# Four-layer graph kernel on one Trainium2 core: the layers' VectorE programs without loops, some masks moved to VectorE, unread TensorE products, another tail of the neighbour maximum

## The chip, the cores and the metric

The kernel runs on one core of a Trainium2 chip. Its time is the device time of one execution in microseconds (us); lower is better. Three runs of the kernel before gave 5988.77 us in the median, 5978.95 and 5993.84 at the ends. The profile is one further execution, traced by the hardware profiler. Engines: PE is TensorE (matrix products, with PEld its weight loads), DVE is VectorE, ACT is ScalarE, POOL is GpSimd, SP is SyncE, which here only issues DMAs.

## The reference

There are N = 8192 nodes with 128 features and a symmetric 0/1 adjacency `adj` of 8192 x 8192 int32 with about 0.4% of ones. Four layers follow one another, each as `x = layernorm(x + layer(x))`:

```
L0: out[i] = max over neighbours j of x[j]        (0 where a row has no neighbour)
L1: h = x @ W;  e = leaky_relu(h@a_src [:,None] + h@a_dst [None,:], 0.2)
    att = softmax(where(adj > 0 and sum(h) != 0, e, -1e9))
    att kept only where att >= 1e-4, times the number of valid neighbours
    out = elu(h + att @ h)
L2, L3: h = x @ W;  the same e;  att = softmax(where(adj > 0, e, -big));  out = elu(att @ h)
```

## The kernel before, in words

**Neighbour maximum** (`neighbour_max`). Rows of `adj` come in 64 tiles of 128 rows, four pieces of 1 MB each (`adjb`, SP's queue). PE transposes a tile in 64 blocks, ACT turns them into 0/1 bytes (`stage`) and stores them as the mask `mask_t` that the later layers read. DVE works out for every row which neighbours are to be gathered one by one, POOL gathers them from a copy of x (`x_ext`) into `ring`, DVE reduces them into `nm` (which is `X`). For the others, PE multiplies "lone" masks with x split in three bf16 parts (`xs`); each product of two blocks is a *pair* (L548): DVE keeps the running maximum `top`. Tiles go in *quads* of four: 16 quads (NC) of 32 pairs; pairs of quad q run beside the tiles of quad q+1, and those of the last quad alone, in a last stretch without new tiles. x itself is loaded in four quarters at the start, by SP, ahead of the second tile's rows; DVE splits them (`SPLIT_BEHIND`: quarter 0 behind tile 1, quarters 1 and 2 behind tile 2, quarter 3 behind tile 3). After the last pair DVE finds each row's lowest value over all 64 tiles (L706), does a few small steps on [128, 64], POOL reduces one flag over the partitions (L352), and DVE and SP read it and branch: if it is set, a slow exact loop runs (it is not set for these inputs). Then `first_norm`, a block of its own, loads x again (SP), multiplies nm by "has neighbours", adds x (L767) and takes the rows' statistics (L769, L772).

**A layer** (`attention_layer`) has a preparation and a main block. In the *preparation* PE transposes X in 16 groups g of four blocks (L886), ACT copies them to `XT` (L909), and PE multiplies them with three columns (L877, four groups behind). In layers 1 and 2 DVE normalises X first (L924, from stats that ACT turned into rstd). In layers 2 and 3 DVE sums all of XT (`zc`, L951) once the last group is copied, and then the preparation ends with a few small steps.

The *main block* goes over 16 chunks c of 512 columns, and in each over 64 tiles j. For each j DVE makes a weight tile `w` = max(q, E[j]) * mask (L1503 in layers 2 and 3; in layer 1 `u` from the threshold theta, L1478, and then w, L1489), in a ring of 8 tiles, and PE multiplies it with GX (L1258). At fixed j (36 and 48 in layer 1, 24, 28 and 38 in layers 2 and 3) DVE handles the results of the chunk before (`post`, `post_rest`, `standardise`).

Layer 1 also needs theta of chunk c+1 while chunk c is multiplied. For each of its 64 tiles PE *lifts* scores (two products of 512 columns, L1186 and L1187, into one of two banks), ACT makes a 0/1 mask of them (`above`, a ring of ten slots, L1322), and PE multiplies masks in batches of eight with `kg` and `km` (L1194, L1196). After the 64th ACT and PE work out theta (L1344 is its last step). For chunk 0 this happens alone, ahead of everything (PE `ahead_of(0, 0, [0, 0], T)`), while DVE has only GX to weigh (L1462); for the others PE mixes it between the products of chunk c.

**What sets the order.** Every engine's program is in order; semaphores link them. In the layers' main blocks the chunks 1 to 14 are a hardware loop of two chunks each on every engine (`chunks`), with chunk 0 and chunk 15 outside. In such a loop a wait's value stands in a register: `Tally` adds to it (L134) and `hold` waits on it (L78) and bumps a spare semaphore. `Steps` waits on constants. The neighbour maximum is written out without loops on PE, ACT and DVE.

## Time and profile before

| | |
|---|---|
| median of three runs | 5988.77 us (5978.95 to 5993.84) |
| profiled execution | 6010.32 us; its trace spans 6008.3 us |
| busy: PE, DVE, ACT, POOL | 5075.2 (84%), 4748.3 (79%), 2028.6 (34%), 1186.8 us (20%) |
| PE's granted clock, mean | 0.922 of 2.4 GHz |
| neighbour maximum with its tail and the first norm | 0 to 2316.7 us |
| layer 1: preparation, theta of chunk 0, the chunks | 2316.7, 2380, 2445 to 4037 us |
| layer 2: preparation, the chunks | 4037, 4091 to 5026 us |
| layer 3: preparation, the chunks | 5026, 5071 to 6008 us |

The stages can be told apart by lines: a stage is between the first and last instruction of its lines. The clock has two levels, 1.2 and 2.4 GHz, and is given as a share of 2.4 GHz: 0.50 is the lower level all the time.

### The profile page before, as it was taken

Reading aid. Unit: us, or ns where it says so; the run is one execution under the profiler, and the core shown is the slowest. Engines: PE = TensorE matmul, PEld = TensorE weight load, DVE = VectorE, ACT = ScalarE, POOL = GpSimd, SP = SyncE. Lnnn points to the kernel's source line nnn. Section 1 sums busy time; section 2 is a strip of 40 time slices with the busy share of each in tenths; the row PEclk is TensorE's granted clock in tenths of the full one; section 3 lists DMA queues with packets and bytes.
Section 4 is the critical chain, followed back from the end, with each engine's and each line's share of the span. In section 5 each row is a group of like instructions: output and inputs, shape, how many; then the busy total and the mean of one; then the engine's idle time right before and its main releaser. Section 6 shows DMA issues by size and latency. Waiting matters only on the chain. (4 is left out here: it accounts for less than half of the span.)

```text
span 6008.3 us, 91716 instructions
## 1 busy us (share of the span) xinstructions
PE 5075.2 (84%) x24003; PEld 2392.2 (40%) x24113; DVE 4748.3 (79%) x8829; ACT 2028.6 (34%) x2862; POOL 1186.8 (20%) x1368
## 2 busy tenths in 40 slices
PE   4777767667677674899999999979999998999999
PEld 3333333333333332344444444435444445444444
DVE  6676766667666665699989998988888886888888
ACT  3444444444444441555555555510000001000000
POOL 5555454454444540000000000000000000000000
PEclk6888888888888885999999999998999998999999
DMA  7555555555555522011111111011222211221211
GB/s 256 191 189 190 188 187 180 178 189 187 184 185 181 184 94 85 29 43 44 44 43 43 44 44 44 29 44 63 72 76 74 73 49 71 74 82 67 89 60 35
DMA packets 149498, 628.30 MB, mean 105 GB/s; under 512 B 29360, under 2 KB 37936, under 8 KB 91632
## 3 DMA queue, kind: packets, MB, share of 16 engines
q1 hardware_dynamic: 78432, 482.58, 23.0%
q0 software_dynamic: 33744, 73.21, 4.1%
q10 hardware_dynamic: 36864, 67.13, 3.2%
q8 instruction: 200, 3.28, 0.2%
q14 instruction: 258, 2.11, 0.1%
HBM read 551.42 MB, written 75.56 MB: 104 GB/s over the span
## 5 line engine op out<-in xcount | busy, mean ns | idle before, releaser
L1258 PE MATMUL bank<-w,GX 128*128 128x512 f32 x6144 | 2777.6, 597 | 41.9 <-DVE w L1489 22.3
L1258 PEld LDWEIGHTS bank<-w,GX 128*128 128x128 f32 x6144 | 1145.6, 190 | 1398.2 <-issue 1340.4
L1503 DVE SCALAR_TENSOR_TENSOR w<-q,E,m 128x512 f32<-128x512 f32 x2048 | 1455.0, 758 | 170.0 <-PE bank L1258 92.0
L306 POOL DMA_INDIRECT ring<-x_ext,idx x1051 | 1030.4, 980 | 1098.1 <-DVE X L560 338.4
L450 PE MATMUL sums<-lone,xs 128*128 128x512 fp8e4 x3000 | 852.3, 427 | 300.9 <-DVE top L548 204.3
L548 DVE TENSOR_TENSOR top<-top,sums 128x1024 f32<-128x1024 f32 x484 | 589.8, 1219 | 645.2 <-remote 378.2
L375 ACT ACTIVATE stage<-tp 128x1024 fp8e4<-128x1024 uint16 x512 | 523.9, 1025 | 1089.9 <-remote 634.7
L1478 DVE SCALAR_TENSOR_TENSOR u<-theta,E,m 128x512 fp8e4<-128x512 f32 x1024 | 765.9, 749 | 98.3 <-issue 84.9
L1322 ACT ACTIVATE above<-bank,offset 128x512 fp8e4<-128x512 f32 x1024 | 649.0, 684 | 529.3 <-PE bank L1187 527.0
L1489 DVE SCALAR_TENSOR_TENSOR w<-q,E,u 128x512 f32<-128x512 f32 x1024 | 760.6, 744 | 74.9 <-PE bank L1258 74.8
L450 PEld LDWEIGHTS sums<-lone,xs 128*128 128x128 bf16 x3000 | 295.2, 106 | 827.4 <-issue 619.0
L362 ACT ACTIVATE lone<-first_ps 128x1024 fp8e4<-128x1024 f32 x512 | 522.1, 1020 | 91.4 <-remote 41.8
L436 PE MATMUL first_ps<-stage,firsts 128*128 128x512 fp8e4 x1022 | 343.2, 421 | 126.3 <-ACT lone L362 99.0
L417 PE MATMUL tp<-ident_b,adjb 128*128 128x128 bf16 x4096 | 361.4, 237 | 76.7 <-issue 40.5
L1187 PE MATMUL bank<-m,lift 128*128 128x512 fp8e4 x1024 | 390.1, 381 | 7.3 <-ACT parts L1300 1.1
L1186 PE MATMUL bank<-parts,three 128*128 128x512 bf16 x914 | 348.5, 381 | 13.0 <-ACT above L1322 12.9
L1134 POOL TENSOR_TENSOR lone_part<-mean_w,nohas 128x512 f32<-128x512 f32 x32 | 37.8, 1185 | 1626.6 <-DVEq L1429 1608.7
L1273 ACT ACTIVATE num<-bank 128x512 f32<-128x512 f32 x48 | 28.4, 592 | 890.9 <-PE bank L1258 890.9
L417 PEld LDWEIGHTS tp<-ident_b,adjb 128*128 128x128 bf16 x4096 | 278.1, 107 | 111.0 <-issue 54.3
L429 PE MATMUL tally<-powers,stage 128*128 128x16 bf16 x4096 | 171.4, 171 | 157.9 <-ACT stage L375 112.6
L429 PEld LDWEIGHTS tally<-powers,stage 128*128 128x128 fp8e4 x4096 | 164.5, 99 | 286.0 <-ACT stage L375 143.5
L553 DVE TENSOR_TENSOR ring<-ring 128x128 f32<-128x128 f32 (+2 forms) x448 | 248.2, 554 | 2.6 <-issue 0.2
(231 smaller groups left out, 3018.2 us busy)
## 6 DMA issues: line engine op xcount, KB each, us to landing
adjb<-in_adj SPq DMA_DIRECT2D x256, 1024.0 KB
m<-mask_t SPq DMA_DIRECT2D x192, 1024.0 KB, 4.9
mask_t<-stage ACTq DMA_DIRECT2D x256, 256.0 KB
ring<-x_ext,idx POOLq DMA_INDIRECT x1051
out<-X SPq DMA_DIRECT2D x16, 256.0 KB, 2.4
Wn<-in_L_gnn_W SPq DMA_DIRECT2D x3, 64.0 KB, 1.9
A<-in_L_gnn_a SPq DMA_DIRECT2D x6, 0.5 KB, 2.1
X<-in_x SPq DMA_DIRECT2D x4, 0.5 KB, 22.3
```

The source lines that it names most:

```text
L306: pool.indirect_dma_start(ring[:, s, :], None, x_ext, bass.IndirectOffsetOnAxis(ap=idx[:, k, s:s + 1], axis=0)).then_inc(done, 16)
L362: nc.scalar.activation(lone[:, b, :, :], first_ps[:, :, :], ACT.Relu, saturate=False).then_inc(lone_made, 1)
L375: nc.scalar.activation(stage[:, q, e * TRB:(e + 1) * TRB, k * P:(k + 1) * P], tp[e % 2][:, :, :].bitcast(U16), ACT.Sign, saturate=False).t ...
L417: last = nc.tensor.transpose(tp[e % 2][:, i, :], low_half[:, j // PW, j % PW:j % PW + P], ident_b[:, :])
L450: last = nc.tensor.matmul(out[:, a, :], xs[:, part_, 2 * n + a, :], lone[:, b, a, :], start=(part_ == 0), stop=(part_ == 2))
L548: nc.vector.tensor_tensor(out=top[:, :, :], in0=top[:, :, :], in1=sums, op=ALU.max).then_inc(sums_used, 1)
L1187: nc.tensor.matmul(out[:, :], lift[:, :], m[:, b, j, :], start=False, stop=True).then_inc(lifted, 1)
L1258: last = nc.tensor.matmul(acc[b][:, :], GX[:, j, :], w[:, j % WR, :], start=(j == 0), stop=(j == T - 1))
L1322: nc.scalar.activation(above[:, j % AR, :], lift_ps[j % 2][:, :], ACT.Sigmoid, bias=offset[:, j:j + 1], saturate=False).then_inc(g_made, 1)
L1478: nc.vector.scalar_tensor_tensor(out=u[:, j % 4, :], in0=theta[:, b, :], scalar=E[:, j:j + 1], in1=m[:, b, j, :], op0=ALU.is_le, op1=ALU.m ...
L1489: nc.vector.scalar_tensor_tensor(out=w[:, j % WR, :], in0=q, scalar=E[:, j:j + 1], in1=u[:, j % 4, :], op0=ALU.max, op1=ALU.mult).then_inc ...
L1503: nc.vector.scalar_tensor_tensor(out=w[:, j % WR, :], in0=q, scalar=E[:, j:j + 1], in1=m[:, b, j, :], op0=ALU.max, op1=ALU.mult).then_inc( ...
```

## The change

- The chunks of DVE's main programs in all three layers are written out as Python loops (`written_out`), and so are ACT's; their registers become constants (`Count` for `Tally`). PE, POOL and SP keep their loops.
- In layer 1 some of the `above` masks are made by DVE (`own_mask`), straight from q, E and the mask, with no lifted scores on PE and nothing on ACT: 32 of 64 (the odd ones) for chunk 0, and tiles 8, 24, 40 and 56 for each later chunk, made behind w tiles 12, 24, 34 and 46 of the chunk before. For chunk 0 DVE weighs three eighths of GX ahead of its masks and the rest behind them.
- In each preparation PE gets products that nobody reads (`keep_warm`, 256 bf16 columns each): 20 at the start, 8 behind group 1, 4 behind each of the groups 2 to 15, and 4 behind each of the next three groups' score products; 96 in all.
- At the start, quarters of x are loaded ahead of the rows of the tile behind which DVE splits them, not all ahead of tile 1.
- At the tail of the neighbour maximum, `first_norm` is gone. SP loads x again (into `adjb`) once the last tile is transposed; DVE takes the lowest value quad by quad behind pairs 8 to 22 of the last quad; POOL adds x to each of those 15 quads as it is released; DVE does the last quad itself; ACT writes the flag. DVE takes the statistics before it reads the flag. The multiplication by "has neighbours" moves into the branch.

```diff
+LOWEST_AT = 8
+WARM = 4
+WARM_UP = 20
+WEIGHED_FIRST = 3
+OWN_FIRST = tuple(range(1, T, 2))
+OWN_AT = {12: 8, 24: 24, 34: 40, 46: 56}
+OWN = tuple(OWN_AT.values())
...
+def own_tiles(c):
+
+    return OWN_FIRST if isinstance(c, int) and c == 0 else OWN
...
+class Count:
+
+    def __init__(self, eng, sem, start=0):
+        self.eng, self.sem, self.at, self.n = eng, sem, start, 0
+
+    def wait(self, n=1):
+
+        self.at += n
+        if self.at > 0:
+            self.eng.wait_ge(self.sem, self.at)
...
-            for k in range(XQ):
-                quarter = slice(k * T // XQ, (k + 1) * T // XQ)
-                sp.dma_start(nm[:, quarter, :], x.rearrange("(t p) f -> p t f", p=P)[:, quarter, :]).then_inc(x_in[k], 16)
-            with sp.Fori(1, T) as t:
+
+            def rows(t):
+
                 for h in range(PIECES):
 
                     hold(sp, transposed, (t - 1) * 8 + (h + 1) * HT)
                     sp.dma_start(adjb[:, h, :], adj[bass.ds(t * P, P), h * PW:(h + 1) * PW]).then_inc(adj_in[h], 16)
 
+            for t in range(1, TC):
+                for k in SPLIT_BEHIND[t]:
+                    quarter = slice(k * T // XQ, (k + 1) * T // XQ)
+                    sp.dma_start(nm[:, quarter, :], x.rearrange("(t p) f -> p t f", p=P)[:, quarter, :]).then_inc(x_in[k], 16)
+                rows(t)
+            with sp.Fori(TC, T) as t:
+                rows(t)
+
+            sp.wait_ge(transposed, T * 8)
+            sp.dma_start(x_again, x.rearrange("(t p) f -> p t f", p=P)).then_inc(x_back, 16)
...
+            pool.wait_ge(x_back, 16)
+            for quad in range(NC - 1):
+                at = slice(quad * TC, (quad + 1) * TC)
+                pool.wait_ge(rows_step, quad + 1)
+                nc.gpsimd.tensor_tensor(out=nm[:, at, :], in0=nm[:, at, :], in1=x_again[:, at, :], op=ALU.add).then_inc(x_added, 1)
...
+            act.wait_ge(missed_shared, 1)
+            nc.scalar.activation(flag[:, :], missed_all[:, :], ACT.Copy).then_inc(flag_ready, 1)
...
+            def lowest_of(quad):
+
+                at = slice(quad * TC, (quad + 1) * TC)
+                rows_done.did(nc.vector.tensor_reduce(lowest[:, at], nm[:, at, :], axis=AXX, op=ALU.min))
+
+            def between(n):
+
+                if n == LOWEST_AT:
+                    dve.wait_ge(top_used, NC - 1)
+                    dve.wait_ge(lower_free, T - TC + 1)
+                    dve.wait_ge(rest_free, T - TC + 1)
+                if LOWEST_AT <= n < LOWEST_AT + NC - 1:
+                    lowest_of(n - LOWEST_AT)
+
+            def row_statistics():
+
+                rows_done.settle()
+                dve.wait_ge(x_added, NC - 1)
+                for t in range(T):
+                    rows_done.did(nc.vector.bn_stats(bn[:, t, :], nm[:, t, :]))
+                rows_done.settle()
+                for t in range(T):
+                    rows_done.did(nc.vector.bn_aggr(stats[:, t, :], bn[:, t, :]))
+                rows_done.settle()
...
                     if quad is not None:
                         pair(quad * 32 + 8 * k + e, 8 * k + e, quad == NC - 1)
+                    if quad == NC - 1:
+                        between(8 * k + e)
...
-            dve.wait_ge(lower_free, T + 1)
-            dve.wait_ge(rest_free, T + 1)
             merge(NC - 1)
             take_top(NC - 1)
             dve.wait_ge(top_used, NC)
-            lowest = junk
-            steps.do(nc.vector.tensor_reduce(lowest, nm[:, :, :], axis=AXX, op=ALU.min))
+            steps.settle()
+            side.settle()
             steps.did(nc.vector.scalar_tensor_tensor(out=due[:, :], in0=due[:, :], scalar=TOP_BIT, in1=found[:, :], op0=ALU.mult, op1=ALU.not_equal))
+            lowest_of(NC - 1)
+            rows_done.settle()
+            dve.wait_ge(x_back, 16)
+            last = slice(T - TC, T)
+            rows_done.did(nc.vector.tensor_tensor(out=nm[:, last, :], in0=nm[:, last, :], in1=x_again[:, last, :], op=ALU.add))
...
-            dve.wait_ge(missed_shared, 1)
-            nc.vector.tensor_copy(flag[:, :], missed_all[:, :]).then_inc(flag_ready, 1)
+            steps.do(nc.vector.tensor_scalar(nohas[:, :], deg[:, :], 0.0, None, ALU.is_equal))
+            row_statistics()
...
-def first_norm(nc, x, X, deg, nohas, stats):
...
+                def keep_warm(number):
+
+                    halves = ident[:, :].bitcast(BF16)
+                    for _ in range(number):
+                        nc.tensor.matmul(banks[5][:, 0:2 * P], halves[:, 0:P], halves, start=True, stop=True)
+
+                keep_warm(WARM_UP)
                 for g in range(NG):
...
                     if g >= BEHIND:
                         scores(g - BEHIND)
+                    if g >= 1:
+                        keep_warm(2 * WARM if g == 1 else WARM)
                 for g in range(NG - BEHIND, NG):
                     last = scores(g)
+                    if g < NG - 1:
+                        keep_warm(WARM)
...
+        def written_out(chunk, end, say_last=False):
+
+            for c in range(NC):
+                if say_last and c == NC - 1:
+                    chunk(c, c % 2, False, True)
+                else:
+                    chunk(c, c % 2, c == 0)
+            end(NC - 1, 1)
...
                 while state[0] < scores or (scores == T and state[1] < T):
                     if state[0] < T:
-                        lifted_scores(c, b, state[0])
+                        if state[0] not in own_tiles(c):
+                            lifted_scores(c, b, state[0])
                         state[0] += 1
...
                 for j in range(T):
...
-                    above_free.wait()
-                    hold(act, lifted, c * T + j + 1)
-                    nc.scalar.activation(above[:, j % AR, :], lift_ps[j % 2][:, :], ACT.Sigmoid, bias=offset[:, j:j + 1], saturate=False).then_inc(g_made, 1)
+                    slots += 1
+                    if j in own_tiles(c):
+                        continue
+                    above_free.wait(slots)
+                    slots = 0
+                    hold(act, lifted, act_tiles_before(c, j) + 1)
+                    nc.scalar.activation(above[:, j % AR, :], lift_ps[lift_bank(c, j)][:, :], ACT.Sigmoid, bias=offset[:, j:j + 1], saturate=False).then_inc(g_made, 1)
...
-            w_free = Tally(dve, w_used)
-            post_steps = Tally(dve, post_step)
+            w_free = Count(dve, w_used)
+            post_steps = Count(dve, post_step)
...
+            def own_mask(c, b, j):
+
+                hold(dve, q_ready, c + 1)
+                hold(dve, mask_in[b][j // QJ], wait_of(c, b))
+                hold(dve, g_used, c * T + j + 1)
+                nc.vector.scalar_tensor_tensor(out=above[:, j % AR, :], in0=qb[:, b, :], scalar=E[:, j:j + 1], in1=m[:, b, j, :],
+                                               op0=ALU.is_le, op1=ALU.mult, saturate=False).then_inc(own_made, 1)
...
                 if first:
-                    for i in range(T // GXP if cut else 1):
+                    for i in range(WEIGHED_FIRST if cut else 1):
                         weigh(i)
                 hold(dve, q_ready, c + 1)
                 if cut:
+                    if first:
+                        for j in OWN_FIRST:
+                            own_mask(0, 0, j)
+                        for i in range(WEIGHED_FIRST, T // GXP):
+                            weigh(i)
...
+                        if j in OWN_AT and not last_chunk:
+                            own_mask(c + 1, 1 - b, OWN_AT[j])
...
-            chunks(dve, chunk, end, True)
+            written_out(chunk, end, True)
```

## Rows read from the trace of the kernel before

**Rows 1.** Stretches (stretch, length, then busy us and count of each engine, clock, DMA):

```profile
2317.00:2380.00 63.00, 41.14 (x195) 40.20 (x196) 27.91 (x118) 12.13 (x23) 0.53 (x3) 0.50 0.34 135
...
2445.00:4037.00 1592.00, 1526.93 (x6309) 646.87 (x6414) 1449.14 (x2352) 806.13 (x1366) 42.33 (x80) 0.99 0.11 38
```

**Rows 2.** Timeline, start of the program (start, length, engine, line, count, idle before and releaser):

```profile
3.01 29.09 SPq L262 DMA_DIRECT2D X<-in_x  x4
...
41.74 1.89 PE L417 MATMUL tp<-ident_b,adjb 128*128 128x128 bf16 x16 [22.49 <-DMA adjb<-in_adj]
...
53.48 0.69 DVE L598 TENSOR_TENSOR keys<-tally,opens 128x512 int32<-128x512 int32 x1 [13.65 <-ACT opens L368]
```

**Rows 3.** Timeline, last pairs of the neighbour maximum to the preparation:

```profile
2238.25 1.22 DVE L548 TENSOR_TENSOR top<-top,sums 128x1024 f32<-128x1024 f32 x1 [0.51 <-PE sums L450]
...
2253.58 8.69 DVE L706 TENSOR_REDUCE stats<-X 128x64 f32<-128x8192 f32 x1
...
2263.54 0.38 POOL L352 PARTITION_ALL_REDUCE missed_all<-missed  x1 [46.98 <-DVE missed L711]
...
2272.15 0.20 DVE L763 TENSOR_SCALAR nohas<-deg 128x64 f32<-128x64 f32 x1 [8.04 <-PEq L164]
...
2298.20 11.89 DVE L769 BATCH_NORM_STATS2 bn<-X 128x6 f32<-128x128 f32 x61
...
2316.70 0.06 DVE L930 MEMSET epsc<- 128x1 f32 x1 [1.68 <-PEq L102]
```

**Rows 4.** POOL's line 1134, all of it (duration min/median/max ns, first and last start):

```profile
L1134 POOL TENSOR_TENSOR lone_part<-mean_w,nohas x32: 1147/1155/1478, 4098.4 to 5899.9; 128x512 f32<-128x512 f32 x32
```

**Rows 5.** Timeline, preparations of layers 1 and 3:

```profile
2320.79 1.97 PE L886 MATMUL bank<-ident,X 128*128 128x128 f32 x8 [67.97 <-DVE X L924]
...
5036.70 0.60 ACT L909 ACTIVATE XT<-bank 128x512 f32<-128x512 f32 x1 [0.69 <-PE bank L886]
...
5057.78 0.60 ACT L909 ACTIVATE XT<-bank 128x512 f32<-128x512 f32 x1 [1.86 <-PE bank L886]
5058.48 8.69 DVE L951 TENSOR_REDUCE zc<-XT 128x1 f32<-128x8192 f32 x1 [26.81 <-ACT XT L909]
```

**Rows 6.** Timeline of ACT, layer 1, masks of chunk 0:

```profile
2426.22 5.43 ACT L1322 ACTIVATE above<-bank,offset 128x512 fp8e4<-128x512 f32 x8 [0.74 <-PE bank L1187]
2432.46 4.04 ACT L1322 ACTIVATE above<-bank,offset 128x512 fp8e4<-128x512 f32 x6 [0.82 <-PE bank L1187]
```

**Rows 7.** ACT's line 1344, theta, all of it:

```profile
L1344 ACT ACTIVATE theta<-bank x16: 597/597/598, 2444.4 to 3931.9; 128x512 f32<-128x512 f32 x16
```

**Rows 8.** Timeline, three thetas of layer 1 and DVE between the second and third:

```profile
2639.56 0.60 ACT L1344 ACTIVATE theta<-bank 128x512 f32<-128x512 f32 x1 [1.07 <-PE bank L1224]
...
2738.28 0.60 ACT L1344 ACTIVATE theta<-bank 128x512 f32<-128x512 f32 x1 [1.04 <-PE bank L1224]
...
2744.60 1.41 DVE L1478 SCALAR_TENSOR_TENSOR u<-theta,E,m 128x512 fp8e4<-128x512 f32 x2 [4.97 <-issue]
...
2838.42 0.60 ACT L1344 ACTIVATE theta<-bank 128x512 f32<-128x512 f32 x1 [1.04 <-PE bank L1224]
```

**Rows 9.** The page's costliest groups: line 1187 (busy us, mean ns, idle before):

```profile
L1187 PE MATMUL bank<-m,lift 128*128 128x512 fp8e4 x1024 | 390.1, 381 | 7.3 <-ACT parts L1300 1.1
```

**Rows 10.** Timeline, layer 2, DVE after the results of a chunk, PE behind it:

```profile
4234.50 0.69 DVE L1439 SCALAR_TENSOR_TENSOR X<-hp,X 128x512 f32 x1 [0.25 <-DVE hp L1437]
...
4236.67 6.71 DVE L1503 SCALAR_TENSOR_TENSOR w<-q,E,m 128x512 f32<-128x512 f32 x10
...
4237.57 2.81 PE L1258 MATMUL bank<-w,GX 128*128 128x512 f32 x6 [0.46 <-DVE w L1503]
```

**Rows 11.** The chain that ended last, layer 3 (start, length, what):

```profile
5162.49 0.86 PE bank L1151 x2
...
5219.88 0.86 PE bank L1151 x2
...
5277.91 0.86 PE bank L1151 x2
```

82 lines of the change are left out of this document (46 added, 36 removed).

## The prediction

> **What bounds the kernel now.** I read the stretches first [rows 1]: they say which engine is full in which stage and at which clock. In layer 1's chunks PE is busy 1526.93 of 1592 us and DVE 1449.14 of 1592, so PE is the bound there with DVE close behind. In its preparation PE is busy 41.14 of 63 us at a clock of 0.50. Then I read the timeline where one stage meets the next, since there engines take turns and every step is on the path: the tail of the neighbour maximum is DVE alone [rows 3], the masks of chunk 0 are an exchange between ACT and PE [rows 6]. Last, the chain that ended last, for the length of a chunk and what interrupts it [rows 11]. The change touches each of these places, so I price seven parts, in time saved on the path, against the profiled execution's 6010.32 us. It lies 21.6 us above the median of the runs, 5988.77 us; I take the saving off that median.
>
> **A. The start: 10 us.** SP is busy for 29.09 us with issuing four quarters of x, 7.3 us each, and only then issues tile 1's rows, for which PE sits idle 22.49 us [rows 2]. With one quarter ahead, they are issued 21.8 us earlier. What follows is DVE, which waits 13.65 us for tile 1's counts and has, from there, 29 us of work in one piece (two extractions and two splits). So at most 13.65 us go; nothing if the DMA engines are simply full (the copy of x into x_ext runs then). I take 10. The moved quarters stand ahead of rows of tiles 2 and 3, whose pieces wait for PE's transposes anyway.
>
> **B. The neighbour maximum's tail: 30 us.** From the lowest value's start to the preparation's first instruction is 2316.70 - 2253.58 = 63.1 us [rows 3]. What remains of it: the lowest value of one quad, 8.69 / 16 = 0.54, with its start 0.6; the last quad's addition, 0.7; six small steps, 1.5; from the statistics' start to the preparation 2316.70 - 2298.20 = 18.5; and the 8.04 us in which DVE reads the flag, branches and leaves the block, which now stand behind the statistics. Together 29.3, so 33.8 go (two passes of 8.69 over all rows and the wait for x, among others). Against it: 15 minima of 0.6 us, 9.0 us of DVE, now stand between pairs. There DVE idles 0.51 us a pair at the end [rows 3], and more before; but it also has the last reductions to do, and PE can run only two sums ahead. I take 3.5 us of delay (0 to 9). POOL's 15 additions cost some 1.16 us each by its nearest row [rows 4], 17 us, and lie in the 46.98 us in which POOL waits for nothing but DVE [rows 3]. If that cover were gone, the statistics would wait up to 17 us. The new load of x takes the place of adjacency rows that have run out. Net 30 (22 to 34).
>
> **C. Preparations: 17.5 us.** At the lower clock a group of four blocks takes 1.86 + 0.60 = 2.46 us; at full clock, which layer 3's preparation had for a short while behind unbroken transposes, 0.69 + 0.60 = 1.29 us [rows 5]. The unread products have no row. The nearest is the f32 transpose of 128 columns, 1.97 / 8 = 0.25 us at half clock [rows 5]; from the product of 512 columns, 0.38 us at full clock and overlapping its neighbours [rows 9], a 256-column one is at most 0.19. I take 0.22 at half and 0.11 at full clock (0 to 0.25: 0 where it hides behind weight loads). A group then takes 1.29 + 4 x 0.11 = 1.73 us, 0.73 less than now. The question is whether the clock rises. In this trace it stood at full where PE ran dense products, and at half in the preparations, where most products are the three-column ones. The twenty products at the start, and the four behind each group, are dense. I expect it to rise within the first groups and to stay. Twelve groups: 8.8 us. Layer 1: 8, with a little for the rise; the first 20 (4.4 us) hide while DVE normalises (4.1 us from 2316.70 to 2320.79). Layers 2 and 3 end by the sum over XT, 8.69 us, which starts with the last copied group [rows 5], so only what comes before that counts: 6.5 for layer 2, and 3 for layer 3, where X is ready at once, the 20 products stand ahead of everything, and three groups already ran at full clock.
>
> The Trainium skill ("TensorE: Matmul & The Clock Gate", section "What's actually happening") says that the gate opens by how busy the engine has been. Here the profile shows PE busy nearly without a break through the second half of that preparation at 0.50, so by the profile's busy time there would be nothing left for unread products to raise. By that rule they only add their own time; this is rival 1.
>
> **D. Theta of chunk 0: 21 us.** ACT makes eight masks in 2432.46 - 2426.22 = 6.24 us [rows 6]: 5.43 of work and a wait for a batch to free slots. With half of them on DVE, ACT has 2.7 us of work in a batch; DVE has 4 x 0.67 (the price of such an operation: 6.71 / 10 [rows 10]) = 2.7 beside it. The exchange remains: slots come free only with PE's batch. I put a batch at 3.6 us. Six batches at full clock save 15.8; the first two, at half clock and with PE's products the bound, some 2.6 each. Bounds: 8 x (6.24 - 3.1) = 25, and 12 if DVE, which starts behind three weighings (3.5 us), sets the pace. The five weighings behind the masks (6 us) lie beside the 7 us of small steps that lead to theta.
>
> **E. Layer 1's chunks: 32 us.** Fifteen thetas apart are 3931.9 - 2444.4 = 1487.5 us [rows 7], 99.17 each. Inside a loop round a chunk takes 2738.28 - 2639.56 = 98.72, with the jump back 2838.42 - 2738.28 = 100.14 [rows 8]: DVE stands for 4.97 us without a cause in the profile, and its ring of eight w tiles covers all but 1.4. Seven jumps on DVE: 10. Four tiles fewer to lift are 8 products of 512 columns; at 0.215 us (at most 0.38 [rows 9]) 1.72 us a chunk, 26 in all. DVE gets 4 x 0.67 = 2.7 us a chunk [rows 10]. In work per chunk, by the shares of [rows 1], DVE goes from 0.910 x 99.2 = 90.3 to 93.0 us and PE from 0.959 x 99.2 = 95.1 to 93.4. The two then sit side by side, so I take 4 off the 36: 32 (10 to 38). An own mask waits for its slot of `above`; behind it on DVE are w tiles, of which PE has up to eight in hand.
>
> **F. Layers 2 and 3: 17 us.** In every chunk PE runs dry once, 0.46 us, behind DVE's handling of the last chunk's results [rows 10]. In that stretch each dependent step of DVE starts 0.25 us after its predecessor, because its wait goes through a register; with constants I expect about 0.1, and with six such steps that is 0.9 us, enough to close the gap. 30 gaps of 0.46: 13.8. The jump back: 5277.91 - 5219.88 = 58.03 against 57.39 [rows 11], so 0 to 0.64 for each of fourteen; I take 3.5 in all. Then PE is full, and nothing is left.
>
> **G. Layer ends: 2 us**, for some five dependent steps of DVE at each of three ends, 0.15 each.
>
> Sum: 10 + 30 + 17.5 + 21 + 32 + 17 + 2 = 129.5 us; 5988.77 - 129.5 = 5859, which I give as 5860.
>
> **Rivals.**
> 1. The clock stays at half in the preparations. For it: PE's busy share there is already near full. Against: what fills it are weight loads. The products then cost 0.22 each: 76 in layer 1, 64 in layer 2 (up to the last copied group), 84 in layer 3, 49 us instead of a gain of 17.5. Time: 5860 + 66 = 5926.
> 2. DVE becomes layer 1's bound: its own masks and the waits for their slots eat what PE saves. For it: 93.0 and 93.4 us of work side by side. Against: DVE's steps get cheaper by constants. Then E is only the jumps, 10: 5882.
> 3. The two ends of the neighbour maximum absorb the edits: the start is bound by the DMA engines (A = 0), and the minima between pairs all count (9, not 3.5): 5860 + 10 + 5.5 = 5876.
> 4. Slower: the written-out programs of DVE stall where the loops did not. The stall of 4.97 us at a jump costs 1.4 us. Were there three such stalls in each of the 48 chunks, that is 144 x 1.4 = 202 us: 5860 + 202 = 6062. It decides from two in each chunk on (134 us). Against it: the chunks outside the loops already are straight code, on the same engines, and so is the neighbour maximum.
>
> **How the numbers follow.** Chances: my forecast 0.66, rival 1 0.12, rival 2 0.10, rival 3 0.09, rival 4 0.03. The parts' own bounds, taken together, give 5838 to 5890 around the forecast; rivals 2 and 3 lie within, and rival 1, with other parts at their better ends, reaches down to 5912. Range 5838 to 5912. 0.3% (18 us) is what a measurement of this kernel can tell from no change: faster 0.95, same 0.02, slower 0.03.
>
> **What would show it.** A: tile 1's first transposes near 20 to 32, not 41.74. B: a preparation that starts some 30 us sooner than by A alone, with POOL's additions done before the last pair. C: clock near 1 and copies of XT 1.7 us apart; 3.3 or so means rival 1. D: about 3.6 us a batch, theta 0 some 44 us into its stage, not 65. E: thetas 97 us apart without a long step every second chunk; 98.7 means rival 2. F: posts 56.9 us apart and no idle of PE ahead of L1258. The prediction is wrong if idle "issue" time shows up inside DVE's written-out chunks, or if the last pairs come over 9 us later.

## The result and the profile after

The changed kernel takes 5835.4 us (median of four runs, 5833.0 to 5839.7), the kernel before beside it 5987.3 us (5979.0 to 5993.8): ratio 0.9748, 95% interval 0.9736 to 0.9761. I had said 5860 with a range of 5838 to 5912. The direction was right, and so was the sign of every part that could be measured; the saving was 152 us instead of 129, and the time lies 2.6 us below the range. Run beside the kernel before on two chips once more, it had the ratio 0.9748 again (e5, e17 below).

The stages, from the start times of their first and last instructions in the two traces (epsilon's memset, the copy of sdh, the thetas). The profiled execution of before stood 23 us above the median of before, that of after at its own median. The stages from the preparations on agree to about 1 us from one execution to the next, apart from layer 1's preparation (up to 3 us, see e1 below); the neighbour maximum doesn't, so I put most of this excess there. Row A is therefore not read from the two traces but is the rest of the 151.9 us.

| stage | before | after | saved | forecast |
|---|---|---|---|---|
| A, neighbour maximum up to the last tile's counts | | | 8.7, as the rest | 10 |
| B, last counts to last pair | 87.5 | 89.5 | -2.0 | -3.5 |
| B, lowest value to preparation 1 | 63.1 | 22.3 | 40.8 | 33.8 |
| C, preparations 1, 2, 3 up to sdh | 48.3, 50.1, 41.0 | 38.6, 39.7, 37.1 | 9.8, 10.4, 3.8 | 8, 6.5, 3 |
| D, sdh to first theta | 79.4 | 59.5 | 19.9 | 21 |
| E, fifteen thetas | 1487.5 | 1452.3 | 35.1 | 32 |
| F and G, sdh to the stage's end, layers 2 and 3 | 938.5, 940.8 | 926.2, 928.9 | 12.3, 11.9 | 19 with the next |
| G, last theta to preparation 2 | 106.1 | 104.9 | 1.2 | |

Stretches of after, in order: the steady part of layer 1's preparation, layer 1's chunks, one chunk of layer 2 (stretch, length, busy us and count of PE, PEld, DVE, ACT, POOL, then PE's granted clock, DMA share, GB/s).

```profile
2262.00:2280.00 18.00, 18.00 (x173) 17.58 (x173) 6.78 (x27) 6.57 (x11) 0.00 (x0) 1.00 0.53 219
2345.00:3798.00 1453.00, 1420.90 (x6121) 613.03 (x6121) 1392.00 (x2248) 767.32 (x1301) 51.60 (x79) 1.00 0.12 42
4040.00:4097.00 57.00, 57.00 (x141) 25.67 (x140) 52.04 (x87) 3.04 (x6) 1.15 (x1) 1.00 0.21 74
```

Against [rows 1], the preparation is at clock 1.00 and no longer at 0.50, and PE has no idle time in this stretch of layer 2. (The same holds from 4000 to 4850 us in layer 2 and from 4960 to 5800 us in layer 3, where it is shown busy all the time.) Layer 1's chunks are 97.8% PE and 95.8% DVE.

The start, which answers to [rows 2]: SyncE, PE, DVE.

```profile
18.16 21.25 SPq L332 DMA_DIRECT2D X<-in_x  x2
39.46 5.50 SPq L327 DMA_DIRECT2D adjb<-in_adj  x4
...
26.26 1.89 PE L494 MATMUL tp<-ident_b,adjb 128*128 128x128 bf16 x16 [7.00 <-DMA adjb<-in_adj]
34.46 1.03 PE L494 MATMUL tp<-ident_b,adjb 128*128 128x128 bf16 x8 [6.31 <-DMA adjb<-in_adj]
...
44.04 0.69 DVE L704 TENSOR_TENSOR keys<-tally,opens 128x512 int32<-128x512 int32 x1 [4.18 <-ACT opens L443]
```

Tile 1's first piece comes at 26.26 instead of 41.74, DVE's wait is 4.18 instead of 13.65.

The tail, which answers to [rows 3]:

```profile
2224.91 0.68 DVE L655 TENSOR_REDUCE codes<-X 128x4 f32<-128x512 f32 x1
2225.62 0.69 DVE L816 TENSOR_TENSOR X<-X,adjb 128x512 f32<-128x512 f32 x1
...
2227.32 0.38 POOL L427 PARTITION_ALL_REDUCE missed_all<-missed  x1 [19.10 <-DVE missed L820]
2227.82 0.20 ACT L481 ACTIVATE flag<-missed_all 128x1 int32<-128x1 f32 x1 [8.11 <-POOL missed_all L427]
...
2242.88 1.26 DVE L674 BATCH_NORM_AGGREGATE stats<-keys 128x2 f32<-128x6 f32 x18
...
2247.16 0.06 DVE L1026 MEMSET epsc<- 128x1 f32 x1 [3.01 <-PEq L131]
```

From the last aggregate to the preparation 3.01 us pass, in which DVE reads the flag, branches and leaves the block. I had set down 8.04 us for these three, and 1.68 for leaving the block that is gone. The sequencers' own records, which the views above leave out, show why. Among them each engine has a DRAIN at the end of a block, ahead of the barrier at which the engines meet. Before:

```
2263.45  8.412 POOL DRAIN L164
2263.54  0.380 POOL PARTITION_ALL_REDUCE L352 missed_all<-missed
```

After:

```
2227.23  8.409 POOL DRAIN L219
2244.18  0.541 DVE TENSOR_LOAD L827 <-flag
2244.76  0.217 DVE FUSED_REGOPS L827
2245.08  0.072 DVE COMPARE_BRANCH L828
2245.68  0.063 DVE DRAIN L219
```

DVE has its flag in 1 us. GpSimd's drain at the block's end takes 8.4 us, and the block's barrier waits for it. Before, everyone waited: DVE had its flag at 2265.13 us and its own drain at 2265.29, GpSimd's drain ended at 2271.86, and DVE went on at 2272.15. Now the drain lies beside 16.8 us of statistics.

The preparation's groups, which answer to [rows 5]:

```profile
2262.63 0.42 PEld L969 LDWEIGHTS bank<-ident 128*128 128x128 bf16 x4
2262.74 0.60 PE L969 MATMUL bank<-ident 128*128 128x256 bf16 x4
2263.07 0.47 PEld L978 LDWEIGHTS bank<-ident,X 128*128 128x128 f32 x4
2263.18 0.60 PE L978 MATMUL bank<-ident,X 128*128 128x128 f32 x4
2263.50 0.97 PEld L962 LDWEIGHTS bank<-U,XT 128*128 128x128 f32 x8
2263.61 0.95 PE L962 MATMUL bank<-U,XT 128*128 128x3 f32 x8
2263.81 0.60 ACT L1005 ACTIVATE XT<-bank 128x512 f32<-128x512 f32 x1 [1.09 <-PE bank L978]
...
2265.49 0.60 ACT L1005 ACTIVATE XT<-bank 128x512 f32<-128x512 f32 x1 [1.09 <-PE bank L978]
```

A group is 1.68 us of PE: 0.44 of unread products (2262.74 to 2263.18), 0.43 of transposes, 0.81 of three-column products.

Theta, all of it, which answers to [rows 7], and the chain in layer 3, which answers to [rows 11]:

```profile
L1459 ACT ACTIVATE theta<-bank x16: 597/597/597, 2345.2 to 3797.5; 128x512 f32<-128x512 f32 x16
```

```profile
5148.76 0.89 PE bank L1281 x8
...
5205.44 0.89 PE bank L1281 x8
...
5262.13 0.89 PE bank L1281 x8
```

(3797.5 - 2345.2) / 15 = 96.82 us a chunk in layer 1, 56.69 in layer 3, where I had 97 and 56.9.

### The profile page after: what moved, and what is told of

It is laid out like the page before. It is cut to its first block and busy times, and to the rows that moved or that the text cites. A ratio compares the mean times of both kernels' runs of the same rounds, so it can differ in the third digit from the quotient of the medians.

```text
span 5834.3 us, 79990 instructions
## 1 busy us (share of the span) xinstructions
PE 4992.9 (86%) x24217; PEld 2360.2 (40%) x24217; DVE 4827.5 (83%) x8933; ACT 1973.8 (34%) x2771; POOL 1219.1 (21%) x1383
## 5 line engine op out<-in xcount | busy, mean ns | idle before, releaser
L1631 DVE SCALAR_TENSOR_TENSOR w<-q,E,m 128x512 f32<-128x512 f32 x2048 | 1483.9, 761 | 144.4 <-PE bank L1367 39.4
L527 PE MATMUL sums<-lone,xs 128*128 128x512 fp8e4 x3000 | 836.4, 420 | 261.4 <-DVE top L625 162.7
L1435 ACT ACTIVATE above<-bank,offset 128x512 fp8e4<-128x512 f32 x932 | 593.2, 683 | 531.1 <-PE bank L1293 530.7
L1293 PE MATMUL bank<-m,lift 128*128 128x512 fp8e4 x932 | 354.4, 380 | 0.0
```

The lines of the kernel that those rows point to most:

```text
L527: last = nc.tensor.matmul(out[:, a, :], xs[:, part_, 2 * n + a, :], lone[:, b, a, :], start=(part_ == 0), stop=(part_ == 2))
L1435: nc.scalar.activation(above[:, j % AR, :], lift_ps[lift_bank(c, j)][:, :], ACT.Sigmoid, bias=offset[:, j:j + 1], saturate=False).then_inc ...
L1631: nc.vector.scalar_tensor_tensor(out=w[:, j % WR, :], in0=q, scalar=E[:, j:j + 1], in1=m[:, b, j, :], op0=ALU.max, op1=ALU.mult).then_inc( ...
```

## The experiments

All are the changed kernel with an edit, apart from e5 and e17, which are the changed kernel as it is. Times are told by stages, since those are sharp to a microsecond or less, while the neighbour maximum shifts by up to 30 us between executions and chips (L724, a few us behind the counts of a tile, started for the last tile between 2137 and 2168 us in fifteen traces that have the changed order of loads, e13 to e15 aside). Ratios are against the kernel before, on the same chip, with 95% intervals. On the chip of e1 to e8 the changed kernel took 5861.4 us (e5) and the kernel before 6010 to 6012. The medians of e1 to e4 and e6 to e8 were 5910.4, 5898.2, 5881.4, 5878.3, 5875.7, 5866.6 and 5871.7 us. Their distances from e5 differ by 2 to 8 us from what the stages below give, less than the neighbour maximum's own spread.

**The unread products left out.**

```
-WARM = 4
-WARM_UP = 20
+WARM = 0
+WARM_UP = 0
```

> Leaves the products that nobody reads out of the three preparations, all else as in the changed kernel. Theory (the unread products are what keeps TensorE's granted clock up there): the preparations go back to what they took before, from the memset of epsilon to the copy of sdh 48.3, 50.1 and 41.0 us instead of 38.6, 39.7 and 37.1, so 24 us in all and a time of about 5859; the copies of a group 2.46 us apart instead of 1.68. Rival (the preparations gained from the statistics being there and from the order at the block's start, not from the clock): under 8 us back, a time below 5844.

Ratio 0.9838 (0.9819 to 0.9857), 5910.4 us, 49 us above e5, where the theory had 24. Preparations 48.3, 50.1 and 41.3 us: the theory for the preparations to 0.3 us. PE in a stretch of the first one, and the copies:

```profile
2280.00:2310.00 30.00, 29.34 (x143) 29.25 (x142) 3.70 (x16) 5.37 (x9) 0.00 (x0) 0.50 0.13 54
```

```profile
2296.15 0.60 ACT L1005 ACTIVATE XT<-bank 128x512 f32<-128x512 f32 x1 [1.86 <-PE bank L978]
2298.60 0.60 ACT L1005 ACTIVATE XT<-bank 128x512 f32<-128x512 f32 x1 [1.86 <-PE bank L978]
```

PE is shown busy 29.34 of 30 us and has 0.50, while the changed kernel has 18.00 of 18.00 and 1.00: what "busy" shows doesn't tell the clock. In layer 1's preparation the changed kernel does not always do equally well: in the trace of after the clock rose 5.6 us into the stage, was at 0.50 again from 9.0 to 12.5 us, and the stage took 38.6 us (38.7 in e5). In e17, the same kernel, it stayed up from 3.2 us on, and the stage took 35.7.

Of the rest of the loss, 16 us were not expected and are found; some 8 us of the medians are not. The 16 us are in layer 1's chunks: every second one was 1.8 to 4.5 us longer, with a standstill of PE inside its own loop, between two products that wait for nothing:

```profile
3055.76 0.22 PE L1265 MATMUL bank<-ident,now 128*3 128x128 bf16 x1
3058.61 0.33 PE L1265 MATMUL bank<-ident,now 128*3 128x128 bf16 x3 [2.63 <-issue]
```

The six standstills are 12.1 us of the 16. In the changed kernel one of 1.11 us was the longest, in e5, the same kernel, 0.83, and in e17 none was over 0.5. e14, e15 and e16 below have it again in every second chunk. Taking instructions out of one stage moves the later code of this engine, and that may move the stall; that the place of the code is the cause is only argued.

**Fewer unread products**, the 20 at the start alone, and two a group instead of four.

```
 e9:  -WARM = 4  +WARM = 0
 e10: -WARM = 4  +WARM = 2
```

> Of the unread products only the 20 at each preparation's start stay; those behind the groups go. Theory (without them TensorE's granted clock falls back among the groups, as the products that are left are short): copies of a group 2.45 us apart, preparations 46 to 50, 47 to 50 and 39 to 41 us. Rival (the first 20 open the clock and the groups' own products keep it): the groups are shorter than with them, 1.68 less 4 products of 0.107 = 1.25 us, and the preparations 4 to 6 us shorter than now, 33, 34 and 32 us.

> Two unread products behind each group instead of four. Theory (their number sets the length of a group as long as the clock stays at its upper level): copies 1.47 us apart, each preparation 3 us shorter: 36, 36.5 and 34 us, 9 us in all, layers else unchanged. Rival (the clock needs them all): it is at its lower level for most of the preparations, 2.2 to 2.45 us a group and 45 to 50 us a preparation, 25 us slower in all.

e9: ratio 0.9787 (0.9751 to 0.9823), preparations 47.2, 48.9, 41.8 us: the clock falls back among the groups; the theory. e10: ratio 0.9776 (0.9726 to 0.9827), preparations 51.9, 53.5 and 34.7 us. Its first and its third preparation:

```profile
2290.00:2320.00 30.00, 30.00 (x152) 29.31 (x152) 5.04 (x20) 5.97 (x10) 0.00 (x0) 0.50 0.28 116
4930.00:4945.00 15.00, 14.58 (x136) 14.21 (x137) 0.92 (x5) 6.40 (x11) 0.00 (x0) 1.00 1.01 423
```

```profile
2294.39 0.60 ACT L1005 ACTIVATE XT<-bank 128x512 f32<-128x512 f32 x1 [2.20 <-PE bank L978]
2297.19 0.60 ACT L1005 ACTIVATE XT<-bank 128x512 f32<-128x512 f32 x1 [2.20 <-PE bank L978]
```

Two at the lower level, where PE is again shown busy without a break, are the worst of all, 2.80 us a group; at the upper level they are the best, 1.46. The four runs took 5889, 5893, 5849 and 5863 us, so by their times and clocks (0.928, 0.926, 0.932, 0.932) some preparations seem to get the upper clock and some don't; only the first of the four was traced. Both theory and rival hold, by turns. With four products the steady groups stood 1.68 us apart in all 48 preparations of the sixteen traces that have them: certainty, for 0.2 us a group.

**VectorE's programs: loops, and registers without loops.**

```
 e2: -w_free = Count(dve, w_used)        (and post_steps, u_done)
     +w_free = Tally(dve, w_used)
     -written_out(chunk, end, True)
     +chunks(dve, chunk, end, True)
 e3: the Tally lines alone
```

> VectorE's programs of the three layers back in loops with counts in registers (ScalarE's stay written out, masks and all else as in the changed kernel). Theory: TensorE's stall in each chunk of layers 2 and 3 comes back at its full cost of 0.69 us (start to start 1.06 instead of 0.43, less than half of it shown as idle), 30 of them, and the jumps with 1 to 2 us a layer: about 12 us in each of layers 2 and 3. Layer 1 loses between 4 us (7 jumps of 0.6) and 18 us (1.2 a chunk). Time 5863 to 5880. Rival (a stall costs the idle that the profile shows, 0.46): 7 to 8 us in each of layers 2 and 3.

> VectorE's programs written out as in the changed kernel, but its counts kept in registers, so that each wait is a register addition, a wait on the register and an increment of a spare semaphore again. Theory: the stall of TensorE once a chunk in layers 2 and 3 comes from these waits in the step behind the chunk before, so it comes back whole: 0.69 us a chunk, 10 us in each layer, and the loops add only the jumps (this run stands 2 to 8 us below the one with loops). Time 5855 to 5872. Rival (the loops' fetching of instructions is what costs): this run is within 4 us of the changed kernel, 5835 to 5840.

e2: ratio 0.9820 (0.9799 to 0.9840), 5898.2 us; layers 2 and 3 +11.6 and +10.9 us, layer 1's chunks 97.38 us (+8.4). e3: ratio 0.9789 (0.9767 to 0.9811), 5881.4 us; layers 2 and 3 +8.7 and +8.4, layer 1's chunks 96.67, no longer than with constants. In layer 2, the kernel before first (the eight products ahead of the gap in [rows 10]), then e2, then e3:

```profile
4233.51 3.60 PE L1258 MATMUL bank<-w,GX 128*128 128x512 f32 x8
```

```profile
4118.78 2.81 PE L1367 MATMUL bank<-w,GX 128*128 128x512 f32 x6 [0.46 <-DVE w L1631]
```

```profile
4118.32 2.81 PE L1367 MATMUL bank<-w,GX 128*128 128x512 f32 x6 [0.27 <-DVE w L1631]
```

The idle time is 0.46 as in [rows 10], and 0.27 without the loop; the chunk is 57.38 and 57.19 us long, against 56.69. So an idle of 0.46 costs 0.69, and one of 0.27 costs 0.50. The products start every 0.43 us, and the trace draws each 0.60 us long. So a gap shows 0.17 less than it is: in the trace of before the starts on its two sides are 1.05 us apart, 0.62 too many, where 0.46 is shown. The next product starts 0.50 us behind instead of 0.43, which is the other 0.07. The Trainium skill ("Perfetto Trace Analysis", section "Tensor Engine Instruction (MATMUL, LD_WEIGHTS)") says that the end which the profiler reports for such an instruction is computed, from its size and a delay of SBUF. The trace agrees in that the drawn products overlap by 0.17 us.

Of the 22.5 us in layers 2 and 3, the register waits are 17.1 and the loops 5.4. The loops' part is for the most part not the jump: their gap is 0.69 instead of 0.50. In e2 and before, the sequencer has register operations of its own (FUSED_REGOPS) ahead of `X<-hp,X`, in e3 it has none, and DVE's idle time before this step is 0.24 us in the kernel before and in e2, 0.15 in e3, and 0.03 in the changed kernel. The theory held (it had 24), the rival of 0.46 a stall didn't.

**No masks by VectorE for chunks 1 to 15, and none for chunk 0.**

```
 e4: -OWN_AT = {12: 8, 24: 24, 34: 40, 46: 56}
     +OWN_AT = {}
 e6: -OWN_FIRST = tuple(range(1, T, 2))   +OWN_FIRST = ()
     -WEIGHED_FIRST = 3                   +WEIGHED_FIRST = 8
```

> VectorE makes no masks for layer 1's chunks 1 to 15 (chunk 0's 32 stay): ScalarE makes all 64 of them again. Theory (four masks a chunk taken off ScalarE and off TensorE's lifting products are worth more than written-out programs in layer 1): 4 pairs of lifting products of 0.213 us each less, 4 times 0.43 = 1.7 us a chunk, so 15 chunks come back by 25 us, 98.5 us from theta to theta, time 5861. Rival 1 (VectorE bounds layer 1 now: it idles 3.7 of 96.8 us, TensorE 1.7): without 4 masks of 0.67 us VectorE has 2.7 us less, TensorE 1.7 more and the chunk stays within 0.5 us: time 5828 to 5843. Rival 2 (nothing is bound by either): no change within 2 us.

> VectorE makes no masks for layer 1's chunk 0 (and weighs all of X at once there, as before the change); four masks in each later chunk stay. Theory (the masks made ahead of theta are what shortened the stretch from the copy of sdh to the first theta from 79.4 to 59.5 us): it goes back to 79 us, time 20 us above the changed kernel's on this chip. Rival (the clock, up when chunk 0 begins, shortened it): it stays below 65 us.

e4: ratio 0.9779 (0.9762 to 0.9796), thetas

```profile
L1459 ACT ACTIVATE theta<-bank x16: 597/597/598, 2370.8 to 3844.1; 128x512 f32<-128x512 f32 x16
```

which is 1473.3 us instead of 1452.3: 21.0 for the masks, 1.4 a chunk; PE was the bound, the theory with 0.3 us a chunk less. With e2's 8.4 for the loop, 29.4 of the 35.1 us are found. The other 5.7 stand in every chunk: 98.72 us inside a loop round before, 98.32 in e4, 0.4 a chunk. What takes them is open; VectorE's registers don't (e3), and ScalarE's program, which no run put back, is among what is left. e6: ratio 0.9785 (0.9765 to 0.9805), from

```profile
2301.18 0.36 DVE L1051 COPY sdh<-bank 128x192 f32<-128x192 f32 x1 [16.92 <-PE bank L962]
```

to the first theta at 2381.33 it took 80.1 us instead of 59.5. All of D is the masks on VectorE, with the order of the weighings that goes with them; none of it is the clock.

**The flag behind the statistics**, then with an all-reduce early in the program, and with a drain early.

```
 e7:  -            nc.vector.tensor_reduce(missed..., op=ALU.max).then_inc(missed_ready, 1)
                   steps.do(... nohas ...)
                   row_statistics()
      +            nc.vector.tensor_reduce(missed..., op=ALU.max).then_inc(missed_ready, 1)
 e8:  e7, and on GpSimd ahead of the gathers
      +            sel_steps.do(nc.gpsimd.memset(missed[:, :], 0.0))
      +            sel_steps.do(nc.gpsimd.partition_all_reduce(missed_all[:, :], missed[:, :], ...))
 e13: e7, and on GpSimd
      +            pool.drain()
                   pool.wait_ge(missed_ready, 1)
```

> The maximum over the rows' misses, its all-reduce on GpSimd and the flag moved behind the row statistics. Theory (GpSimd's drain of 8.4 us behind the all-reduce holds the barrier, and the statistics covered it): from the last aggregate to the memset of epsilon 3.0 us becomes 3.0 + 0.3 for the reduction + about 9.5, 12 to 13 us; time 9 to 10 us above the changed kernel's. Rival (what I predicted: VectorE's reading of the flag took the 8.04 us, which goes with any flag): as VectorE reads the flag behind the statistics in both kernels, only the hops are added, 1.5 us.

> As the kernel with the flag late, and one more all-reduce of a cleared tile on GpSimd at its start, before the gathers. The drain took 8.4 us behind the first all-reduce of the execution and 0.5 us behind that of each preparation. Theory (it is the first use that costs): the drain at the end is 0.5 us and the stretch from the last aggregate to the memset of epsilon is 4 to 5 us, so most of what the late flag costs is gone. Rival (it is what GpSimd did before, gathers and additions, that has to drain): it stays at 12 to 13 us.

> As the kernel with the flag late (10.1 us from the last aggregate to the memset of epsilon, GpSimd's drain at the block's end 8.41 us), with one more drain on GpSimd, written ahead of its wait for the misses, beside VectorE's statistics. Theory (what the drain of 8.4 us clears is bookkeeping of this engine's own transfers, the gathers of this block, which the preparations' blocks don't have): the drain ahead takes 8.4 us there, the one at the block's end 0.5 us, and the stretch falls to 3.4 to 4 us. Rival (any drain behind an all-reduce at the end of this block takes 8.4 us): it stays at 10.1 us.

e7, ratio 0.9766 (0.9749 to 0.9784):

```profile
2263.84 0.22 DVE L822 TENSOR_REDUCE missed<-rstd 128x1 f32<-128x64 f32 x1
2264.20 0.38 POOL L427 PARTITION_ALL_REDUCE missed_all<-missed  x1 [34.49 <-DVE missed L822]
2264.69 0.20 ACT L481 ACTIVATE flag<-missed_all 128x1 int32<-128x1 f32 x1 [25.20 <-POOL missed_all L427]
...
2273.94 0.06 DVE L1026 MEMSET epsc<- 128x1 f32 x1 [9.88 <-PEq L131]
```

From the last aggregate's end it is 10.13 us instead of 3.01, 7.1 more, where the rival had 1.5; the drain holds the barrier. The expected 12 to 13 counted the drain behind the leaving; part of the 3.01 runs beside it. e8 (0.9768, 0.9751 to 0.9786): 10.13 again, drain 8.41; the first use isn't the cause, and my theory there fell. e13 (0.9740, 0.9724 to 0.9756):

```profile
1727.41 0.38 POOL L428 PARTITION_ALL_REDUCE missed_all<-missed  x1 [34.48 <-DVE missed L823]
...
1731.11 0.06 DVE L1027 MEMSET epsc<- 128x1 f32 x1 [3.84 <-PEq L131]
```

```
1691.61  9.251 POOL DRAIN L426
1727.31  0.552 POOL DRAIN L219
```

The early drain takes the time (9.25 us), the last one 0.55 us, the stretch 4.10. So what the first drain of this block pays for, the second doesn't pay again. GpSimd's additions aren't the reason, since the kernel before has none there and its drain took 8.41 us too. That it is the bookkeeping of the gathers, I only infer: the preparations' blocks have no transfer of GpSimd's, and their drains behind the same kind of all-reduce took 0.5 us.

**The quarters of x ahead of the rows, as before.**

```
+            for k in range(XQ):  (the four loads)
             for t in range(1, TC):
-                for k in SPLIT_BEHIND[t]:  (the loads)
                 rows(t)
```

> SyncE loads the four quarters of x ahead of the second tile's rows, as before the change. Theory (the quarters ahead of the rows delay the start of the counting alone): the second tile's first transposes of TensorE at 41 us instead of 26, the second tile's count on VectorE 7 to 10 us later, and the last count of the neighbour maximum 5 to 10 us later; stages from the preparations on unchanged. Rival (the delay is made up before the last tile, as VectorE bounds the steady part and its later start is absorbed): last count within 3 us. As the neighbour maximum differs from chip to chip and by some us from one execution to the next, the places of the counts in the trace tell more than the time.

Ratio 0.9774 (0.9739 to 0.9808). DVE's counts of the second tile:

```profile
55.10 0.69 DVE L704 TENSOR_TENSOR keys<-tally,opens 128x512 int32<-128x512 int32 x1 [15.27 <-PE tally L506]
```

11 us later than 44.04. At first the lag shrank: for L724 it was 11 us at the second tile, 8 at the third and 5 at the ninth (287.2 us against 277 to 287, mean 282, in the fifteen others). Further on, the others differ too much among themselves: at the 25th tile the counts of e11 came 14 us behind their mean and 5 behind the last of them, at the 64th 12 behind the mean and 3 ahead of the last. The last L724 was at 2164 us, within what the other order gives. Whether any of it lasts to the end is open; the 10 us of A were not shown.

**More masks a chunk.**

```
 e12, e18: OWN_AT = {11: 6, 20: 18, 29: 30, 38: 42, 47: 56}   (tile 54 in the expectation of e12 is 56 here)
 e14:      OWN_AT = {10: 5, 17: 15, 24: 25, 31: 35, 38: 45, 46: 55}
 e15:      OWN_AT = {9: 4, 15: 12, 20: 20, 26: 28, 32: 36, 38: 44, 44: 52, 49: 60}
 e16:      OWN_AT = {9: 4, 15: 12, 26: 28, 32: 36, 38: 44, 49: 60}
```

> Five masks by VectorE in each later chunk of layer 1 instead of four (tiles 6, 18, 30, 42, 54). Theory (TensorE still bounds layer 1): 0.43 us less for TensorE's two lifting products, a chunk of 96.4 instead of 96.83, 6 us less in the layer. Rival (VectorE bounds it by now: 93.1 us of work in 96.8): VectorE's work grows by 0.67 and the chunk by up to 0.67 instead, 97.0 to 97.5, up to 10 us more.

> Six masks by VectorE in each later chunk of layer 1 (four: 96.83 us a chunk, five: 96.40). Theory (TensorE bounds the chunk as long as VectorE's work, 92.8 us with four masks and 0.67 for each more, is below it): VectorE 94.1, the chunk 95.97 us, 13 us less than with four over the layer. Rival (VectorE's waits for TensorE's products, which come at fixed places, leave it no room): 96.4 or more.

> Eight masks, one in each group of eight tiles. TensorE alone would need 96.83 less 4 times 0.43 = 95.1 us a chunk, VectorE's work is 92.8 + 4 x 0.67 = 95.5 us beside its own waits of 1 to 2 us. Theory (VectorE bounds the chunk from here): 96.0 to 97.5 us a chunk, no better than six. Rival (its waits vanish when it is the one that is late): 95.5 us, 20 us less than with four over the layer.

> Six masks a chunk again, but for tiles that VectorE can make without waiting for TensorE's next group of eight denominators (4, 12, 28, 36, 44, 60; in the eight-mask kernel these waited once a chunk, 2.0 us, and the shortest chunks took 94.96 us; in the first six-mask kernel the mask of tile 25 waited 3.0 us in every chunk and TensorE waited for it). Theory (not the number but that wait made six masks slower): 95.9 to 96.0 us a chunk apart from chunks with a stall of TensorE at its loop's row terms, 10 to 13 us less than with four masks over the layer. Rival (six are too many for VectorE): 97 us or more again.

Chunks from theta to theta: five masks 96.40 (most of them), exactly one pair of lifting products less; e12's ratio 0.9746 (0.9706 to 0.9786). Six (e14, 0.9765, 0.9749 to 0.9781) 97.8, and 99.0 to 99.9 in five more, as in every chunk one mask waited for PE's group of eight denominators, and PE then for the mask:

```profile
2561.83 0.75 DVE L1584 SCALAR_TENSOR_TENSOR above<-q,E,m 128x512 fp8e4<-128x512 f32 x1 [3.01 <-PE bank L1304]
```

Eight (e15, 0.9739, 0.9722 to 0.9755) 94.96 in the good chunks, 99.1 to 100.1 in every second one, with PE's standstill in its loop again (2.4 to 3.5 us; 1.7 to 3.1 in e14):

```profile
2509.40 0.38 PE L1265 MATMUL bank<-ident,now 128*3 128x128 bf16 x4 [2.44 <-issue]
```

Six at other tiles (e16) 95.97 to 96.01, and some 97.1 in every second one, with standstills of 1.0 to 1.3 us. So the place made e14 slow, not the number. In chunks without the standstill PE still bounds layer 1 with eight masks (94.96 us, eight lifting products less than with four), where I had expected VectorE to take over. Over the whole stage eight gained nothing, 1450.6 us.

**The changed kernel on other chips.**

> The changed kernel once more, beside the three that follow on the same chip. In the first four experiments the kernel before took 24 us longer than elsewhere, all of it in the neighbour maximum, so absolute times are only compared with this run's. Theory: the stages are those of the first execution to 0.5 us: preparations 38.6, 39.7 and 37.1, 96.8 us from theta to theta, 926.2 and 928.9 us behind the preparations of layers 2 and 3; ratio to the kernel before 0.974 to 0.976.

> The changed kernel on this chip, as the measure for the two kernels with more masks. On the last chip the neighbour maximum took 500 us less in all kernels while the other stages stood; ratio to before 0.972 to 0.976 by the saving of 140 to 150 us there or 152 here.

> Five masks a chunk once more, beside the changed kernel. Theory: 96.40 instead of 96.83 us a chunk and no stalls of TensorE at its loop, 6.5 us below the changed kernel; with six at 95.97 us it would be 13, which the stalls of the loop may take back.

e5: 5861.4 us against 6010.3, ratio 0.9748 (0.9731 to 0.9765), stages as forecast. On one more chip, side by side, five runs each: the changed kernel 5837.4 us, 0.9748 (0.9735 to 0.9762); five masks 5832.2 us, 0.9740 (0.9727 to 0.9753); six at other tiles 5833.0 us, 0.9738 (0.9725 to 0.9752). By the traces the fifteen intervals, the changed kernel first, then five masks, then six:

```profile
L1459 ACT ACTIVATE theta<-bank x16: 597/597/597, 2344.6 to 3795.6; 128x512 f32<-128x512 f32 x16
```

```profile
L1459 ACT ACTIVATE theta<-bank x16: 597/597/598, 2345.1 to 3789.6; 128x512 f32<-128x512 f32 x16
```

```profile
L1459 ACT ACTIVATE theta<-bank x16: 597/597/598, 2349.3 to 3793.9; 128x512 f32<-128x512 f32 x16
```

1451.0, 1444.5 and 1444.6 us. Five masks save 6.5 us in the stage and 5.2 in the medians, but the intervals of the ratios overlap: a gain that only the trace shows.

## Why the prediction missed, step by step

- **A** (10): as the rest of the sum it is 8.7 us; e11 shows 11 us at the second tile and 5 at the ninth, and can't tell what is left at the last. Not confirmed; that 8.7 comes near 10 may be luck.
- **B** (30): measured 38.8. The step that failed: "the 8.04 us in which DVE reads the flag, branches and leaves the block, which now stand behind the statistics". The profile gave the wait to PE's sequencer, [8.04 <-PEq L164], at a barrier where all engines wait for each other, and I took the work of the waiting engine for its cause. It was GpSimd's drain, 8.41 us. It starts with the all-reduce, which the change moves ahead of 16.8 us of statistics, so it is covered: e7 takes that cover away and gives 7.1 us back. In the sum, 8.04 and the last block's leaving, 1.68, should remain behind the statistics; it was 3.01 for both. This is 7 of the 22 us by which the saving was off; with it the range would have begun at 5831 and held the time. The minima between pairs cost 2.0, not 3.5. GpSimd's additions took 1.3 us each for the 1.16 of the nearest row, and were done 13 us ahead of the last pair.
- **C** (17.5): 24.0, and e1 returns 24.4. The mechanism was right: the clock rises, a group takes 1.68 for my 1.73. Mis-sized was layer 2, for which I had 6.5 and measured 10.4: eleven spacings between copies are 0.77 us shorter, 8.5 in all, and the first groups gave another 1.5. I had 8.8 for twelve groups and took 2.3 off because only what comes before the sum over XT counts; but all these spacings lie before it. Rival 1 (the clock stays) is refuted, but e10 shows how near it was: with half the products it was true for two preparations of three in the trace.
- **D** (21): 19.9, and e6 confirms that it is the masks. A batch took 3.86 us (2313.49, 2317.35, 2321.21 in ScalarE's timeline), not 3.6.
- **E** (32): 35.1. Masks 21.0 (I had 26 less 4), the loop of VectorE 8.4 (10), 5.7 not told apart. The 0.215 us for a lifting product had no row behind it; e12's chunks, 0.43 shorter for one pair, bear it out. Rival 2 is refuted twice: e4 shows PE as the bound with no such masks, e12 with five. The pair "93.0 and 93.4 us of work side by side" compared busy times, and they don't say which of the two has slack: in the changed kernel PE was busy 94.7 and DVE 92.8 of 96.8 us a chunk, and taking work off PE still shortened the chunk.
- **F and G** (19): 25.4. The step that failed: "30 gaps of 0.46". The gap's cause and its cure were right: e3 brings 17.1 us back by the registers alone, and a dependent step starts 0.03 us after its predecessor, where I had 0.1. Its price was 0.69 us. 30 times 0.23 is 6.9 us, all of the miss. The jumps back cost what I had set down: in the trace of before the chunks with a jump are 3.4 us longer in all than the 57.38 of the others (I had 3.5).
- Rival 3: the minima cost 2.0 us and not 9, so that half is refuted; the other, A = 0, is open. Rival 4: in the changed kernel no standstill like the 4.97 us at the jump appears inside VectorE's straight chunks.

The errors add: B 8.8, C 6.5, F and G 6.4, E 3.1, against D 1.1 and A 1.3; 22.4 us in all. Four terms were too small, by 9 to 27% of what was measured, each from its own cause. The range reached 22 us below the forecast, about what the better bounds stated for A, B, D, E and F give together. What it had no room for is that B went past its own bound (38.8 against 34) while C, and F with G, each came out 6 us high.

## What to carry to other kernels

Price a gap of TensorE by the starts of its products, or by the length of the whole chunk, not by the idle time shown: 0.46 shown was 0.69 lost. A wait at a block's end that names a sequencer is a barrier; look at every engine's last records, GpSimd's drain above all, before giving the time to one. Work that a fixed wait can lie beside (statistics, here 16.8 us beside 8.4) is worth placing there. When a change relies on the clock, try half of the means too: here half was worse than none in two preparations of three.

## What the runs showed of the hardware that I had not expected

- GpSimd's drain at the end of a block with 1051 gathers: 8.4 us, once. In the preparations' blocks it took 0.5 us, in the layers' main blocks 0.7 to 1.1.
- TensorE in a loop of two chunks stands still at one place, once a round: 1.6 to 3.5 us in e1, e14 and e15, 1.0 to 1.3 in e16, and in the others at most twice in a run and at most 1.3. In e1 no edit lies in that loop; the rounds' longer chunks were 1.8 to 4.5 us longer there. The cause is open.
- On the chip of e13 to e15 the kernel before took 5462.4 us, some 520 to 550 less than on the others, and the three edited kernels 5319 to 5336, with ratios of 0.974 to 0.9765. All of it was in the neighbour maximum: the first preparation began at 1730 to 1732 us, and the later stages stood. A stretch of the changed kernel's steady part and its longest wait, on a usual chip:

```profile
400.00:1200.00 800.00, 564.40 (x4602) 291.18 (x4601) 554.86 (x1219) 384.38 (x428) 404.30 (x448) 0.88 0.56 189
```

```profile
ACT stage L450 <- remote: 241.5, 46, 8.9
```

and the stretch of e14 on that chip:

```profile
400.00:1200.00 800.00, 653.80 (x6143) 354.72 (x6142) 743.44 (x1627) 516.07 (x571) 547.95 (x591) 0.99 0.75 251
```

In the changed kernel's trace ScalarE waits 46 times in 800 us, up to 8.9 us, for something that the trace only calls remote; in the same stretch of e14 it has no such wait, the DMA engines move 251 GB/s instead of 189, and DVE is busy 93% instead of 69%. That the neighbour maximum is bound from outside the core on the usual chips fits this, and would explain why A's gain can't be followed to the end, but no run shows it, and its source is open.
